# A recommendation tower on one NeuronCore: three of its fifteen looked-up tables are gathered instead, and the products of the fourth tile move

## The reference

```python
e = jnp.stack([tbl_0[ids[:, 0]], ..., tbl_25[ids[:, 25]]], axis=1)      # (512, 26, 128)
combined = jnp.concatenate([dense_features[:, None, :], sparse_features], axis=1)
interactions = jnp.einsum('bnd,bmd->bnm', combined, combined)           # (512, 27, 27)
interactions_flat = interactions[:, _TRIU_I, _TRIU_J]
z = jnp.concatenate([dense_features, interactions_flat], axis=1)
h = jnp.concatenate([z, r_dense_features], axis=1)                      # (512, 607)
h = jnp.maximum(h @ W_top1 + b_top1, 0.0)                               # (512, 512)
h = jnp.maximum(h @ W_top2 + b_top2, 0.0)                               # (512, 256)
y = h @ W_top3                                                          # (512, 1)
```

## Time and profile before

| | us |
|---|---|
| median of 3 runs | 121.82 |
| lowest and highest run | 121.16 and 123.47 |
| span of the profiled execution | 118.8 |

### The profile page before, as it was taken

One profiled execution on the slowest core, in us unless ns is written; L12 is line 12 of the kernel. 1 busy time (PEld: TensorE's weight loads), 2 busy tenths in 40 slices (PEclk: granted clock), 3 DMA queues, 4 the chain that ended last, 5 costly groups with the idle time before them and its releaser, 6 DMA issues.

```text
span 118.8 us, 3660 instructions
## 1 busy us (share of the span) xinstructions
PE 110.5 (93%) x1573; PEld 90.3 (76%) x1573; DVE 72.8 (61%) x160; ACT 59.2 (50%) x111; POOL 52.5 (44%) x52
## 2 busy tenths in 40 slices
PE   5999999979999999999997999766999999999991
PEld 2377578848888888888885899654799999999970
DVE  3799999999899997999399700070072053044020
ACT  3729967994497776790999050301020211113441
POOL 2777778778877777778777700000000000000000
PEclk9999999999999999999999999985599999999999
DMA  4899999999996799649942200000000000000000
GB/s 87 283 303 282 279 256 258 246 273 247 268 263 138 199 258 257 159 92 337 397 145 50 61 22 6 6 0 6 6 6 6 6 0 6 6 6 0 0 0 1
DMA packets 6044, 15.48 MB, mean 130 GB/s; under 512 B 1655, under 2 KB 2427, under 8 KB 5902
## 3 DMA queue, kind: packets, MB, share of 16 engines
q1 hardware_dynamic: 4452, 12.20, 36.9%
q0 software_dynamic: 1408, 2.89, 9.9%
q10 hardware_dynamic: 170, 0.18, 0.7%
HBM read 15.26 MB, written 0.00 MB: 129 GB/s over the span
## 4 chain that ended last, share of the span: by engine, by line
PE 83%; DVE 9%; issue 3%; DMA 2%; ACT 1%; DVEq 0%
PE ps_a L355 46%; PE ps_gram L392 10%; DVE onehot L544 6%; PE ps_rows L426 5%; PE ps_h L440 5%; PE ps_a L426 5%; PE ps_rows L370 5%; DMA idrow<-ids_by_table 2%; PE ps_rows L416 2%; PE ps_z L403 2%; PE ps_a L453 2%; DVE part_sb L553 2%; PE ps_a L416 1%; DVE table_sb L571 1%; PE ps_h L466 1%
## 5 line engine op out<-in xcount | busy, mean ns | idle before, releaser
L355 PE MATMUL ps_a<-onehot,part_sb 125*128 125x512 f32 (+1 forms) x272 | 63.6, 386 | 1.9 <-issue 1.7
L327 POOL DMA_INDIRECT rows_sb<-tbl,ids_sb x44 | 51.9, 1179 | 15.3 <-issue 13.1
L355 PEld LDWEIGHTS ps_a<-onehot,part_sb 125*128 125x128 f32 x272 | 47.7, 188 | 13.7 <-issue 4.0
L544 DVE TENSOR_SCALAR onehot<-idrow,row_id 125x512 fp32r<-125x512 int16 (+1 forms) x78 | 42.2, 602 | 2.6 <-DMA idrow<-ids_by_table 1.5
L553 DVE TENSOR_TENSOR part_sb<-table_sb,part_sb 125x512 fp32r<-125x512 f32 (+1 forms) x30 | 20.6, 716 | 2.0 <-ACT part_sb L610 2.0
L571 DVE STREAM_TRANSPOSE table_sb<-ps_gram 128x864 f32<-128x864 f32 x4 | 4.3, 1083 | 26.6 <-PE ps_gram L392 26.6
L631 ACT COPY xt<-ps_a 128x512 f32<-128x512 f32 (+1 forms) x16 | 10.0, 628 | 19.0 <-PE ps_a L355 11.9
L610 ACT CAST part_sb<-table_sb 125x1024 fp32r<-125x1024 f32 (+2 forms) x16 | 16.8, 1056 | 2.7 <-DMA table_sb<-tbl 2.7
L392 PE MATMUL ps_gram<-xt 128*27 128x27 f32 x1024 | 13.1, 201 | 2.8 <-issue 2.1
L392 PEld LDWEIGHTS ps_gram<-xt 128*27 128x27 f32 x1024 | 11.1, 114 | 5.6 <-issue 4.2
L638 ACT COPY xt<-ps_rows 128x128 f32<-128x128 f32 (+2 forms) x32 | 8.2, 340 | 5.6 <-PE ps_rows L370 5.4
(11 more groups left out here) (33 smaller groups left out, 44.4 us busy)
## 6 DMA issues: line engine op xcount, KB each, us to landing
table_sb<-tbl SPq DMA_DIRECT2D x11, 448.0 KB
table_sb<-tbl SPq DMA_DIRECT2D x4, 560.0 KB
idrow<-ids_by_table SPq DMA_DIRECT2D x5, 256.0 KB
w_sb<-w SPq DMA_DIRECT2D x1, 1280.0 KB
rows_sb<-tbl,ids_sb POOLq DMA_INDIRECT x44
table_sb<-tbl SPq DMA_DIRECT2D x10, 52.0 KB
idrow<-ids_by_table SPq DMA_DIRECT2D x4, 128.0 KB
w_sb<-w SPq DMA_DIRECT2D x1, 512.0 KB
```

The costliest lines, as they stand in the source:

```text
L327: pool.indirect_dma_start(rows_sb[:, t % ROWS_RING, GATHERED.index(f), :], None, tables[f], bass.IndirectOffsetOnAxis(ids_sb[:, t, f:f + 1 ...
L355: last = pe.matmul(ps_a[:, (h + piece) % 2, a:b], parts_sb[part][:, w, c * D:(c + 1) * D], unit_onehot(u, c)[:, member, a:b], start=(part ...
L544: dve.tensor_scalar(unit_onehot(u, c), idrow[0:VP, w, 0:n, :], row_id[0:VP, first + c:first + c + 1], None, ALU.is_equal).then_inc(onehot_ ...
```

## The change

- The tables 0, 1 and 7 (1250 rows each, 10 chunks) aren't looked up any more but gathered. Twelve tables are looked up, eleven with 8 chunks and one with 10, in seven units; 14 are gathered, in four groups for each tile (4, 4, 4, 2), 56 gathers in all. POOL's waits for lookups are gone; its wait for the ring of two tiles stays.
- The vectors stand in `xt` in the order dense, looked up, gathered (`ORDER`), so a group is one copy. The rows of the first layer's weights are permuted on the host to match.
- Eight groups are turned beside the lookups, the other eight among the products and layers. PE's order after the lookups is written out: `gram(2, ...)` stands with the layers of tile 0; the layers of tile 1 and nearly all of tile 2's come before the products of tile 3; then come `gram(3, 0..3)` with `layer2(2, ...)` between them, and behind them `layer1_dense(3)`, `turn_z(3)` and `layer1_pairs(3)`.
- Layer 1 uses the two banks of `ps_a` for every tile, so `layer1_dense(t, k)` waits for the `relu1` of tile t-1.

```diff
-ONEHOT_TABLES = [4, 10, 11, 0, 17, 19, 1, 20, 24, 5, 25, 3, 7, 8, 14]
+ONEHOT_TABLES = [4, 10, 11, 17, 19, 5, 20, 24, 25, 3, 8, 14]
-CHUNKS = [8] * 3 + ([10] + [8] * 2) * 4
+CHUNKS = [8] * 5 + [10] + [8] * 6
-UNITS = [[0], [1, 2], [3], [4, 5], [6], [7, 8], [9], [10, 11], [12], [13, 14]]
+UNITS = [[0], [1, 2], [3, 4], [5], [6, 7], [8, 9], [10, 11]]
-GROUP_SIZES = [4, 4, 3]
+ORDER = [0] + [f + 1 for f in ONEHOT_TABLES] + [f + 1 for f in GATHERED]
+FIRST_GATHERED = 1 + NOH
+GROUP_SIZES = [4, 4, 4, 2]
-AFTER_LOOKUP = [[], [], [], [0], [1], [2], [3], [4], [5], [], [6], [7], [8], [9], []]
-BETWEEN_PRODUCTS = [10, 11]
+AFTER_LOOKUP = [[], [], [0], [1], [], [2], [3], [4], [], [5], [6], [7]]
@@ h1_block, h2_block
-            banks = ps_rows if t % 2 else ps_a
-            return banks[:, m // 2, (m % 2) * P:(m % 2 + 1) * P]
+            return ps_a[:, m // 2, (m % 2) * P:(m % 2 + 1) * P]
-            return ps_a[:, m, 0:P] if t == TILES - 1 else ps_h2[:, 0, m * P:(m + 1) * P]
+            if t == TILES - 1:
+                return ps_rows[:, m, 0:P]
+            return ps_h2[:, 0, m * P:(m + 1) * P]
@@ gpsimd
-                    if issued >= GATHERS_AHEAD and (issued - GATHERS_AHEAD) % GATHERS_PER_LOOKUP == 0:
-                        pool.wait_ge(lookup_done, (issued - GATHERS_AHEAD) // GATHERS_PER_LOOKUP + 1)
@@ layer1_dense
-                elif k == 0 and t == 1:
-                    pe.wait_ge(group_copied, len(GROUPS))
-                elif t >= 2:
-                    pe.wait_ge(h1_high_ready if k else h1_low_ready, t - 1)
+                if t:
+                    pe.wait_ge(h1_high_ready if k else h1_low_ready, t)
@@ tensor, after the last lookup's first piece and gram(0, 0), gram(0, 1)
+            turn_group(8)
             gram(0, 2)
             layer1_dense(0, 0)
             gram(0, 3)
             layer1_dense(0, 1)
+            turn_group(9)
             gram(1, 0)
+            turn_group(10)
             gram(1, 1)
+            turn_z(0)
+            gram(1, 2)
+            turn_group(11)
+            layer1_pairs(0, 0)
+            layer1_pairs(0, 1)
+            gram(1, 3)
+            layer1_pairs(0, 2)
+            layer1_pairs(0, 3)
+
+            gram(2, 0)
+            layer2(0, 0)
+            gram(2, 1)
+            layer2(0, 1)
+            turn_z(1)
+            gram(2, 2)
+            turn_group(12)
             layer1_dense(1, 0)
             layer1_dense(1, 1)
+            gram(2, 3)
             for m in range(M1):
+                layer1_pairs(1, m)
+            turn_group(13)
+
+            layer2(1, 0)
+            layer2(1, 1)
+            turn_z(2)
+            turn_group(14)
+            layer1_dense(2, 0)
+            layer1_dense(2, 1)
             for m in range(M1):
+                layer1_pairs(2, m)
+            turn_group(15)
+            gram(3, 0)
+            gram(3, 1)
+            layer2(2, 0)
+            gram(3, 2)
+            gram(3, 3)
+            layer2(2, 1)
+            layer1_dense(3, 0)
+            layer1_dense(3, 1)
+
+            turn_z(3)
+            for m in range(M1):
+                layer1_pairs(3, m)
@@ vector
-            for t in range(2):
-                pack(t)
-            for t in range(TILES):
-                relu1_high(t)
-                if t + 2 < TILES:
-                    pack(t + 2)
+            pack(0)
+            pack(1)
+            relu1_high(0)
+            pack(2)
+            relu1_high(1)
+            relu1_high(2)
+            pack(3)
+            relu1_high(3)
@@ copy_group
-                for slot, n, count in runs(features):
-                    last = act.copy(
+                act.copy(xt[:, t * P // RUN:(t + 1) * P // RUN, slots, :].rearrange("p q n r -> p n q r"),
@@ scalar, after the last copy_lookup
+            for g in (8, 9, 10):
                 copy_group(g)
             copy_z(0)
+            copy_group(11)
+            relu1_low(0)
+            relu2(0)
+            copy_z(1)
+            copy_group(12)
+            relu1_low(1)
+            copy_group(13)
+            relu2(1)
+            copy_z(2)
+            copy_group(14)
+            relu1_low(2)
+            copy_group(15)
+            relu2(2)
+            copy_z(3)
+            relu1_low(3)
```

More of the change, by code:

```diff
@@ L124 @@
 SPQ = NPAD // QUARTERS
-def runs(features):
-    out = []
-    for slot, n in enumerate(features):
-        if out and out[-1][1] + out[-1][2] == n:
-            out[-1][2] += 1
-        else:
-            out.append([slot, n, 1])
-    return out
 def packed_w1(w1):
@@ L143, in packed_w1 @@
         for u in range(TRI):
-            left = N - 1 - (i + u)
-            packed[at + u * length:at + u * length + left] = w1[first_row[i + u]:first_row[i + u] + left]
+            for k, other in enumerate(ORDER[i + u + 1:]):
+                low, high = sorted((ORDER[i + u], other))
+                packed[at + u * length + k] = w1[first_row[low] + high - low - 1]
     chunks = list(packed.reshape(ZC, P, H1)) + [w1[0:D], w1[w1.shape[0] - D:]]
@@ L317, in _ @@
             pool.wait_ge(ids_landed, 16)
-            issued = 0
-            for g, (t, features) in enumerate(GROUPS):
-                if t >= ROWS_RING and t != GROUPS[g - 1][0]:
+            for g, (t, first, n) in enumerate(GROUPS):
+                if t >= ROWS_RING and first == 0:
                     pool.wait_ge(group_turned, GROUPS_UP_TO[t - ROWS_RING])
-                for n in features:
-                    f = n - 1
-                    if issued >= GATHERS_AHEAD and (issued - GATHERS_AHEAD) % GATHERS_PER_LOOKUP == 0:
-                        pool.wait_ge(lookup_done, (issued - GATHERS_AHEAD) // GATHERS_PER_LOOKUP + 1)
-                    issued += 1
+                for k in range(first, first + n):
+                    f = GATHERED[k]
                     pool.indirect_dma_start(
-                        rows_sb[:, t % ROWS_RING, GATHERED.index(f), :], None, tables[f],
+                        rows_sb[:, t % ROWS_RING, k, :], None, tables[f],
                         bass.IndirectOffsetOnAxis(ids_sb[:, t, f:f + 1], 0),
@@ L361, in turn_group @@
             def turn_group(g):
-                t, features = GROUPS[g]
+                t, first, n = GROUPS[g]
                 if g >= 2:
@@ L367, in turn_group @@
                     pe.wait_ge(ident_landed, 16)
-                pe.wait_ge(group_landed[g], 16 * len(features))
-                for slot, n in enumerate(features):
+                pe.wait_ge(group_landed[g], 16 * n)
+                for slot in range(n):
                     last = pe.transpose(ps_rows[:, g % 2, slot * P:(slot + 1) * P],
-                                        rows_sb[:, t % ROWS_RING, GATHERED.index(n - 1), :], ident)
+                                        rows_sb[:, t % ROWS_RING, first + slot, :], ident)
                 last.then_inc(group_turned, 1)
@@ L485, in _ @@
             lookup(NOH - 1, 1, [3])
-            turn_group(BETWEEN_PRODUCTS[0])
+            turn_group(8)
             gram(0, 2)
@@ L694, in _ @@
             copy_lookup(NOH - 1, 1)
[L695 removed]
+            for g in (8, 9, 10):
                 copy_group(g)
             copy_z(0)
[L698 to L703 removed]
+            copy_group(11)
[13 more added lines that the diff above has]
+            relu1_low(3)
             for done in range(TILES - 1):
                 copy_y(done)
[L706 to L707 removed]
+            relu2(TILES - 1)
+            copy_y(TILES - 1)
 _INPUTS = [f"tbl_{f}" for f in range(F)]
```

54 lines of the change are left out of this document (9 added, 45 removed).

## The result

| | before | after |
|---|---|---|
| median, us | 122.16 (4 runs, 121.16 to 123.47) | 109.20 (4 runs, 108.59 to 110.46) |
| span of the profiled execution, us | 118.8 | 107.0 |

The ratio after/before is 0.900, with a 95% interval of 0.892 to 0.908: the changed kernel is faster by 10%. The forecast was 111.6 us, between 108.3 and 115.5.

The account below looks back on a forecast made before the run. PE was taken as the bound, the lookups running at its pace. Span 118.8 - 13.7 + 1.3 (transposes) + 0.8 (start) + 1.6 - 0.4 (order) + 0.2 (issue gaps) = 108.6, plus 3.0 around it: 111.6 us, range 108.3 to 115.5.

Parts of the forecast that it names:

- The bound, and 60 products at 0.228: Lookups run at PE's own pace; three tables fewer take 60 products of 0.228 us, 13.7 us, off PE's stream.
- the rival in which DVE sets the pace: Lookups: removed products don't shorten them because DVE sets the pace instead of PE; 113.6 us, chance 0.04.
- The new start: First lookups, until 13 us: low parts stand behind more and longer comparisons on DVE, +0.8 us, between 0 and 2.
- Gathers: POOL's 12 more gathers at 1.25 to 1.49 us each land before PE wants them; cost nothing, 8.4 at worst row.
- First gram at 57.5: End of lookups: tile 0's first products start at 57.5 us, from 71.4 less 13.7 and 1.0, plus 0.8.
- The new order: Waits before gram(3, 0), turn_z(3) and pairs(3) cost 0.65, 0.35 and 0.6 us, +1.6; turn_group(9) before gram(1, 0) gives back 0.4.
- The half clock: 77 to 87 us: the drop costs 2.8 and was assumed to stay; rival that it goes away, 108.8 us, chance 0.15.
- Gaps of "issue" as late instructions: PE's gaps of 1.04 and 1.09 us in gram(0) and gram(1) read as late instructions; +0.2 us for changes in them.
- The 3.0 us around the span: Median of before's runs lies 3.0 us above its profiled span; carried over, from 108.6 to 111.6 us.
- slower: 0.02: Slower than before if group 15's gathered rows come 10.2 us later than wanted; 124.4 us at 1.8 per gather, chance 0.02.

Follow-up runs that it names:

- after_third: The changed kernel unaltered, run again on chip 12: 149.73 us beside 125.01 for the kernel before.
- the batches: Changed kernel with covered tail and POOL's old lookup waits, gathers from 36 on issued three at a time behind PE's progress, chip 4: 133.43 us, 1.090 of before.
- The covered tail: Changed kernel with dense and pairs work laid beside the exposed waits around gram(3), turn_z(3) and pairs(3), chip 12: 147.27 us, repeated 147.02 us.
- eleven tables: Changed kernel with eleven tables looked up, fifteen gathered, groups 9 to 11 turned later, POOL's old waits back, chip 12: 141.56 us, 1.150 of before.

## Why the prediction was right, and what it did not see

For its own runs the forecast held: faster, 109.2 in a range of 108.3 to 115.5, 2.4 below the value. Part of that is luck, of two kinds: misses of opposite sign cancel within the sum, and the four runs fell on an occasion without a standstill; on chip 12 the same kernel took 149.7. Step by step:

- **The bound, and 60 products at 0.228.** Right. The lookups still run as blocks at PE's pace and DVE kept level, so the rival in which DVE sets the pace falls. The new start cost what was put down for it, 0.8, or a little more: the block that ended at 18.46 before ends at 19.40.
- **Gathers.** Right in kind, and safer than said. The term that was mis-sized is the interval: 1.487 was carried over from a trace with comparisons nearly to the end, while the last 20 here came every 1.25, with no comparison beside them. The first 44 didn't keep their recorded times either: the 44th started at 63.08, not at 67.40. Group 15's data came at about 81, not at 85.0 to 87.8, and PE wanted them at 89.3, not at 92.3: a slack of 8 instead of 4.5 to 7.
- **First gram at 57.5.** It was 55.33. Of the 2.2, 1.5 are two gaps of issue that the old lookups had (0.81 and 0.70) and the new ones don't: the sum put issue gaps at +0.2 in all. The other 0.7 wasn't taken apart.
- **The new order.** 0.65, 0.35 and 0.6 were forecast, 0.47, 0.26 and 0.57 measured; the run of the order alone shows the last two again. The wait of gram(1, 0) kept 0.48 where 0.2 was forecast: its cover by one group was taken for too much. From the first gram to layer 3 the forecast said 45.4 and the trace 101.19 - 55.33 = 45.9. This hides two misses of opposite sign: issue gaps of 3.4 us where the old stretch had 2.1, and 0.84 to 0.99 instead of 0.75, at a granted clock of 1.00, for six of the twelve quarters of gram that have gathers beside them (about +1.1, which no step had), against the half clock that went away.
- **The half clock.** It had a chance of 0.15 to go and is gone in this profile; the time of that rival, 108.8, is close to the 109.2 measured, but not for its reason, since its price of 2.8 us isn't found in other runs. Of seven runs of the kernel before on chip 14, three spanned 118.5 us at a mean clock of 0.971, 119.2 at 1.000 and 119.2 at 0.955: the span doesn't follow the drop. The work in that stretch was counted as if nothing else held it at full clock. What fills it when the clock stays up isn't known; no run took it apart. The order alone kept the half clock, and the old place of gram(1, 0) with its wait didn't bring it back, so what starts it stays open too.
- **Gaps of "issue" as late instructions.** The timing bears this out for the short gaps: the profile lists the transfers of a queue of kind "instruction" (here for the changed kernel: packets, MB, share of the span of 16 engines).

```profile
q8 instruction: 12, 0.20, 0.8%
```

  That is twelve transfers of 16 KB in the changed kernel's span. In the profile of before two end at 76.33 and 81.23, and PE resumes from its gaps at 77.60 and 82.62; in that of the changed kernel they end at 66.37, 78.41 and 92.36, and PE resumes at 67.75, 79.78 and 93.90. In the fourteen profiles every gap of 0.5 us or more in gram that stands outside a standstill or a batch ends 1.3 to 1.6 us behind the end of such a transfer. Only the size was off: 3.4 us where the sum had its +0.2 on top of 2.1. Not every transfer makes a gap, and which do isn't known.
- **The 3.0 us around the span.** The profiled run took 108.8, 1.8 more than its span. The forecast had compared one execution's span with the median of others.

Together, from the forecast's 111.6: -2.2 for the first gram, +0.5 to layer 3, +0.1 behind it and -1.2 for what lies around the span give 108.8, the profiled run's time; the median of the four runs is 0.4 above it.

**The step that failed** is the one behind "slower: 0.02". It asked only whether gathered rows come late, and priced a wait for data. On chips 12 and 4 the kernels with fourteen or more gathered tables were slower by 9 to 20% (2% where half of the gathers were left out), and not because rows were late: in `after_third` POOL itself waited for PE (14.21 us). The gaps of issue were in the trace of before, 1.04 and 1.09 us, and were read as a small constant of the dense products. The change lays some 20 gathers beside those products. Whether the gaps were a sign of what followed isn't shown.

The Trainium skill (Runtime: NRT & Kernel Launch, Instruction fetch mechanics) has each engine fetch its instructions in blocks by a DMA queue of its own, the cost mostly hidden. The short gaps above agree that there are such blocks, but some cost up to 2 us. The standstills are something else. While PE trickles between 80 and 97 us in `after_third`, no transfer of that queue runs, only those of the gathers; with the waits back one ends at 78.0, and the trickle goes on until 90.9 and ends without another. So PE doesn't trickle for want of a block that is on its way, as far as the transfers show. What does hold it, or ACT in the first standstill, no run shows. That the trickle beside gram comes and goes with the gathers is shown, by the batches and by the kernel without late gathers.

**What stays open.** Why ACT stands still within the lookups of the changed kernel on chip 12. Of the kernel before there is no profile on that chip, only its times, which leave no room for a long standstill; its lookups with the new order show a small one (ACT idle for 3.30 us and DVE for 2.46 before 63.1). And why putting the waits back removes it, although in that run POOL was first held at 26.1 us, for 0.61 us only, just when PE's trickle began in `after_third` (at 26.7). Whether it is the chip or the hour: chip 12 showed it in two sets 36 minutes apart, chip 14 and the run of the first result didn't, but chips 14 and 4 were seen only once. The covered tail and eleven tables never ran where nothing stands still, so whether either beats 108 us is not known. No version run here was faster than the changed kernel.

## What to carry to other kernels

Work that leaves the bound engine is worth its full time if what takes its place ends early enough. Check that as here: the interval of the new work, its landing, and the moment at which it is wanted. But ask also what the moved work now runs beside. Indirect gathers beside a dense run of small matmuls are a risk that a single clean profile doesn't show. When an engine stands on "issue" for long, look in the kernel for what its next instruction needs, and whether that had only just been made: here the longest gap of PE was ACT's. Measure such a change on more than one chip before believing a gain, and where the gathers can end before the dense stretch begins, let them.

## What the runs showed of the hardware that was not expected

- The same program took 108.1 us on chip 14 and 149.7 on chip 12, while the kernel before differed by 3% (121.5 and 125.0).
- While GpSimd issues indirect gathers (0.94 us each, 0.30 between), PE can be held to a few instructions every 0.71 us in gram, with the DMA engines only a fifth busy. It recovered 1 to 4 us after the last gather of a stretch.
- PE's gaps of issue in gram outside the standstills end 1.3 to 1.6 us behind the end of a transfer of 16 KB in the profile's instruction queue; in the 17 us of the standstill beside gram (80 to 97 in `after_third`) there is none.
- ACT, too, stood still for 8.7 to 14.9 us with its input made, in five profiles on chip 12, beginning while POOL gathered.
- Even where nothing stands still, 64 products of 27 columns take 0.84 to 0.99 us in six of twelve cases beside gathers at a granted clock of 1.00, and 0.75 without gathers.
- Covering a wait of PE in a dense stretch can lengthen the next gap of issue (0.75 to 1.42 us for 1.04 us of waits).
